# The output stage of a two-layer image kernel: two buffers for its inputs, and the next image's sums among this image's groups

## The reference, cut to what matters

```python
ys = ys + Ds.reshape(1, K_DIRS, d, 1) * xs          # four directions
y = _cross_merge(ys, h, w)                          # flips the reversed two, transposes the column order, adds
y = jnp.transpose(y, (0, 2, 1))                     # pixels first, channels last
mu = jnp.mean(y, -1, keepdims=True)
var = jnp.mean(jnp.square(y - mu), -1, keepdims=True)
y = (y - mu) * jax.lax.rsqrt(var + LN_EPS) * ln_weight + ln_bias
```

## Time and profile before

| | us |
|---|---|
| median of 3 runs | 22312.98 |
| lowest, highest | 22303.36, 22334.86 |
| the profiled execution: its time | 22314.07 |
| the profiled execution: its span | 22312.3 |
| the output stage's part of the span (21397.2 to 22312.3) | 915.1 |

### The profile page before, as it was taken

The page is one execution under the profiler, slowest core; times in us unless marked ns, Lnnn a source line. Parts: engine busy times, 40 slices in busy tenths (PEclk is TensorE's granted clock), DMA queues, the critical chain, the costliest instruction groups (busy, mean ns, idle before and its releaser), DMA issues. The chain is left out here.

```text
span 22312.3 us, 287094 instructions
## 1 busy us (share of the span) xinstructions
PE 16801.2 (75%) x84632; PEld 5876.1 (26%) x84632; DVE 19495.2 (87%) x21108; ACT 9584.4 (43%) x14631; POOL 16107.3 (72%) x5892
## 2 busy tenths in 40 slices
PE   8999999989997777777777777777777777777731
PEld 5555555552221111111111111111111111111111
DVE  5555555559998999999999999999999999999976
ACT  3433433337774444444444444444444444444410
POOL 0000000006667999999999999999999999999977
PEclk9999999999997777777777777777777777766765
DMA  0000000016666666666666666666666666666666
GB/s 20 15 16 16 15 16 15 16 37 226 231 227 154 131 129 126 126 128 128 129 129 131 128 128 126 126 129 130 129 128 128 128 127 125 130 131 129 128 144 163
DMA packets 1129422, 2519.98 MB, mean 113 GB/s; under 512 B 247606, under 2 KB 448824, under 8 KB 1112960
## 3 DMA queue, kind: packets, MB, share of 16 engines
q1 hardware_dynamic: 1128320, 2508.11, 50.2%
HBM read 2000.43 MB, written 507.38 MB: 112 GB/s over the span
## 5 line engine op out<-in xcount | busy, mean ns | idle before, releaser
L1212 POOL TENSOR_TENSOR c_pr<-c_hs,c_c_u 128x1568 f32<-128x1568 f32 x3072 | 10794.1, 3525 | 546.5 <-DVE c_hs L1176 473.0
L1119 ACT ACTIVATE c_psum<-c_dt_u,c_a_neg 128x784 f32<-128x784 f32 x6144 | 5641.7, 918 | 8236.2 <-DVE c_hs L1176 8192.6
L1064 PE MATMUL c_psum<-c_pr,c_red 128*64 128x392 f32 x24576 | 7302.9, 713 | 2.7 <-POOL c_pr L1212 2.7
L1176 DVE TENSOR_TENSOR_SCAN c_hs<-c_psum,c_carry,c_dbx 128x784 f32<-128x784 f32 x3264 | 6347.1, 2025 | 0.0
L1053 PE MATMUL c_psum<-c_br_u,c_sel 48*128 48x512 bf16 (+1 forms) x8704 | 3008.3, 438 | 4148.5 <-DVE c_dbx L1156 4051.7
L1156 DVE TENSOR_TENSOR c_dbx<-c_u_u,c_psum 128x784 f32<-128x784 f32 x4352 | 4857.3, 1116 | 51.7 <-PE c_psum L1053 51.7
L195 POOL TENSOR_TENSOR a_xpb<-a_x_sb,a_pb_sb 98x768 f32<-98x768 f32 x128 | 231.5, 1809 | 4641.0 <-DVE a_x L283 4627.4
L1201 POOL TENSOR_TENSOR c_dbp<-c_u_u,c_bp_u 128x784 f32<-128x784 f32 x1792 | 3334.4, 1861 | 42.3 <-DMA c_c_u<-scr_bc 42.3
L1176 DVE TENSOR_TENSOR_SCAN c_hs<-c_psum,c_carry,c_dbp 128x784 f32<-128x784 f32 x1344 | 2734.2, 2034 | 0.0
L1053 PEld LDWEIGHTS c_psum<-c_br_u,c_sel 48*128 48x128 bf16 x8704 | 524.4, 101 | 8379.4 <-DVE c_dbx L1156 7925.3
L1064 PEld LDWEIGHTS c_psum<-c_pr,c_red 128*64 128x64 f32 x24576 | 1804.3, 178 | 3472.2 <-issue 3188.6
(11 more groups left out here) (117 smaller groups left out, 18555.2 us busy)
## 6 DMA issues: line engine op xcount, KB each, us to landing
c_c_u<-scr_bc SPq DMA_DIRECT2D x512, 1568.0 KB, 28.9
c_dt_u<-scr_dt SPq DMA_DIRECT2D x512, 588.0 KB, 7.4
c_u_u<-scr_u SPq DMA_DIRECT2D x512, 588.0 KB, 11.4
c_bp_u<-scr_bc SPq DMA_DIRECT2D x512, 588.0 KB, 22.2
scr_dt<-p_dt_o SPq DMA_DIRECT2D x384, 392.0 KB, 3.0
scr_u<-p_u_o SPq DMA_DIRECT2D x384, 392.0 KB, 2.4
scr_y<-c_y_sb SPq DMA_DIRECT2D x256, 294.0 KB, 17.8
d_yin<-scr_y SPq DMA_DIRECT2D x32, 2352.0 KB, 14.4
```

The costliest lines, as they stand in the source:

```text
L1064: mm = pe.matmul(Y(3 * w + q)[64 * h:64 * h + 64, :], red[:], pr[:, s % RP, HT * h:HT * h + HT], start=(p == 0 and opens(w)), stop=(p == N ...
L1119: nc.scalar.activation(dA(s), dt_u[:, d, s // NPR, :], ACT.Exp, scale=a_neg[:, k, s:s + 1]).then_inc(exp_done, 1)
L1176: nc.vector.tensor_tensor_scan(hs[:, s % RH, way], dA(s)[:, way], data, init, ALU.mult, ALU.add).then_inc(scan_done, 1)
L1212: nc.gpsimd.tensor_tensor(pr[:, s % RP:s % RP + 2, :], hs[:, s % RH:s % RH + 2, :], c_u[:, d, s % NPR:s % NPR + 2, :], ALU.mult).then_inc( ...
```

## The change

Nothing is computed otherwise. The changes of order and storage are:

- `yin` and `x_in` get a second buffer, by the parity `par` of the image. `yf` is gone: VectorE writes its result in place over plane 0 of `yin`, and TensorE reads it there.
- SP issues both loads of image b+1 at the head of image b's body, behind a wait for the transposes of image b-1 (`t_full`), and then the seven stores of image b. The body is written twice in the loop, once for each parity (`halves`).
- GpSimd's two additions for image b+1 stand behind groups 0 and 2 of image b (`add`), VectorE's two operations for image b+1 behind `normalise(3)` and `normalise(5)` of image b (`with_x`). Those of image 0 stand ahead of everything.
- TensorE waits for the single PSUM banks that it overwrites, and no longer for the whole image before.

```diff
-        yin = sb("yin", [HC, 2, 2, L])
-        x_in = sb("x_in", [HC, 2, L])
-        yf = sb("yf", [HC, 2, L])
+        yin = sb("yin", [HC, 2, 2, 2, L])
+        x_in = sb("x_in", [HC, 2, 2, L])
...
+        def halves(eng, body):
+
+            body(0, 0, False)
+            if n_img > 2:
+                with eng.Fori(0, n_img // 2 - 1) as i:
+                    body(2 * i + 1, 1, False)
+                    body(2 * i + 2, 0, False)
+            body(n_img - 1, 1, True)
...
-            def stores(b):
+            def body(b, par, last):
+                if not last:
+                    if not (isinstance(b, int) and b == 0):
+                        sp.wait_ge(t_full, NGRP * b)
+                    for a in range(2):
+                        load(b + 1, 1 - par, a)
                 for g in range(NGRP):
                     sp.wait_ge(o_done, NGRP * b + g + 1)
                     dst = out[bass.ds(b, 1), TT * GT * g:TT * GT * (g + 1), :].rearrange("u (t p) c -> p (u t) c", p=TT)
                     sp.dma_start(dst, ob[:, g].rearrange("p (t c) -> p t c", t=GT)).then_inc(o_out[g], 16)
 
-            load(0, 0)
-            load(0, 1)
-            if n_img > 1:
-                with sp.Fori(0, n_img - 1) as b:
-                    for a in range(2):
-                        sp.wait_ge(yf_done, 2 * b + a + 1)
-                        load(b + 1, a)
-                    stores(b)
-            stores(n_img - 1)
+            load(0, 0, 0)
+            load(0, 0, 1)
+            halves(sp, body)
...
-            def body(b, first):
-                for a in range(2):
-                    pool.wait_ge(y_in[a], 48 * b + 48)
...
+            def add(b, par, a):
+                pool.wait_ge(y_in[par][a], 24 * (b - par) + 48)
+                rows = yin[:, par, a, 0].rearrange("p (h w) -> p h w", h=IMG)
+                nc.gpsimd.tensor_tensor(rows, rows, yin[:, par, a, 1].rearrange("p (w h) -> p h w", h=IMG),
+                                        ALU.add).then_inc(add_done, 1)
+
+            def body(b, par, last):
                 for g in range(NGRP):
...
                     nc.gpsimd.tensor_tensor(o, o, b_sb[:].unsqueeze(1).to_broadcast([TT, GT, C]), ALU.add).then_inc(o_done, 1)
+                    if not last and g in (0, 2):
+                        add(b + 1, 1 - par, g // 2)
...
-                    if a == 0 and not first:
-                        dve.wait_ge(t_full, NGRP * b)
-                    nc.vector.scalar_tensor_tensor(yf[:, a], x_in[:, a], dsum[:, a:a + 1], yin[:, a, 0],
-                                                   ALU.mult, ALU.add).then_inc(yf_done, 1)
+            def with_x(b, par, a):
+                dve.wait_ge(add_done, 2 * b + a + 1)
+                y = yin[:, par, a, 0]
+                nc.vector.scalar_tensor_tensor(y, x_in[:, par, a], dsum[:, a:a + 1], y, ALU.mult, ALU.add).then_inc(yf_done, 1)
...
                     stat(g)
                     if g:
                         normalise(g - 1)
+                    if not last and g in (4, 6):
+                        with_x(b + 1, 1 - par, g // 2 - 2)
                 normalise(NGRP - 1)
...
-                    elif not first and g < 4:
-                        pe.wait_ge(nm_done, NGRP * b)
+                    elif not (isinstance(b, int) and b == 0):
+                        pe.wait_ge(nm_done, n - (2 if g < 3 else 6))
```

More of the change, by code:

```diff
@@ L1248, in build_output @@
         c_in = sem("d_c_in")
-        y_in = [sem("d_y_in0"), sem("d_y_in1")]
+        y_in = [[sem(f"d_y_in{par}{a}") for a in range(2)] for par in range(2)]
         ready = sem("d_ready")
@@ L1266, in _, with load @@
                 sp.dma_start(dst, src).then_inc(c_in, 16)
-            def load(b, a):
-                sp.dma_start(yin[:, a], ysc[bass.ds(2 * b, 2), a].rearrange("u p t -> p u t")).then_inc(y_in[a], 16)
+            def load(b, par, a):
+                arrived = y_in[par][a]
+                sp.dma_start(yin[:, par, a], ysc[bass.ds(2 * b, 2), a].rearrange("u p t -> p u t")).then_inc(arrived, 16)
                 top = SHIFT * IMG
-                sp.dma_start(x_in[:, a, top:L], xn[a, :, bass.ds(b * L + top, L - top)]).then_inc(y_in[a], 16)
-                sp.dma_start(x_in[:, a, 0:top], xn[a, :, bass.ds(b * L + L, top)]).then_inc(y_in[a], 16)
-            def stores(b):
+                sp.dma_start(x_in[:, par, a, top:L], xn[a, :, bass.ds(b * L + top, L - top)]).then_inc(arrived, 16)
+                sp.dma_start(x_in[:, par, a, 0:top], xn[a, :, bass.ds(b * L + L, top)]).then_inc(arrived, 16)
+            def body(b, par, last):
[4 more added lines that the diff above has]
+                        load(b + 1, 1 - par, a)
                 for g in range(NGRP):
@@ L1303, in _ @@
                 pool.sem_inc(o_out[g], 16)
-            def body(b, first):
-                for a in range(2):
-                    pool.wait_ge(y_in[a], 48 * b + 48)
-                    rows = yin[:, a, 0].rearrange("p (h w) -> p h w", h=IMG)
-                    nc.gpsimd.tensor_tensor(rows, rows, yin[:, a, 1].rearrange("p (w h) -> p h w", h=IMG),
-                                            ALU.add).then_inc(add_done, 1)
+            def add(b, par, a):
[4 more added lines that the diff above has]
+            def body(b, par, last):
                 for g in range(NGRP):
@@ L1317, in body @@
                     nc.gpsimd.tensor_tensor(o, o, b_sb[:].unsqueeze(1).to_broadcast([TT, GT, C]), ALU.add).then_inc(o_done, 1)
-            images(pool, body)
+                    if not last and g in (0, 2):
+                        add(b + 1, 1 - par, g // 2)
+            add(0, 0, 0)
+            add(0, 0, 1)
+            halves(pool, body)
         @block.vector
@@ L1326, in _, with body @@
             dve.wait_ge(ready, 2)
[L1328 to L1331, removed]
-                    if a == 0 and not first:
-                        dve.wait_ge(t_full, NGRP * b)
-                    nc.vector.scalar_tensor_tensor(yf[:, a], x_in[:, a], dsum[:, a:a + 1], yin[:, a, 0],
-                                                   ALU.mult, ALU.add).then_inc(yf_done, 1)
+            def with_x(b, par, a):
+                dve.wait_ge(add_done, 2 * b + a + 1)
+                y = yin[:, par, a, 0]
+                nc.vector.scalar_tensor_tensor(y, x_in[:, par, a], dsum[:, a:a + 1], y, ALU.mult, ALU.add).then_inc(yf_done, 1)
+            def body(b, par, last):
+                first = isinstance(b, int) and b == 0
                 def stat(g):
@@ L1362, in body @@
                         normalise(g - 1)
+                    if not last and g in (4, 6):
+                        with_x(b + 1, 1 - par, g // 2 - 2)
                 normalise(NGRP - 1)
-            images(dve, body)
+            with_x(0, 0, 0)
+            with_x(0, 0, 1)
+            halves(dve, body)
         @block.scalar
@@ L1380, in body @@
                     nc.scalar.activation(rstd[:, g], lnv[:, g], ACT.Exp, scale=-0.5).then_inc(rs_done, 1)
-            images(act, body)
+            halves(act, body)
         @block.tensor
@@ L1398, in body @@
                             tok = TT * (GT * g + t)
-                            mm = pe.transpose(tile_ps(g, t)[:, HC * a:HC * a + HC], yf[:, a, tok:tok + TT], id_sb[:])
+                            mm = pe.transpose(tile_ps(g, t)[:, HC * a:HC * a + HC], yin[:, par, a, 0, tok:tok + TT], id_sb[:])
                     mm.then_inc(t_full, 1)
-            images(pe, body)
+            halves(pe, body)
 def build(nc, ins, out, n_img):
```

## The result

| | before | changed |
|---|---|---|
| median, us | 22305.45 (6 runs) | 22434.76 (6 runs) |
| lowest to highest, us | 22276.27 to 22334.86 | 22416.42 to 22466.75 |
| ratio to before, 95% interval | | 1.006, 1.0047 to 1.0073 |
| profiled execution: time, span | 22314.07, 22312.3 | 22440.55, 22438.7 |
| output stage, from SP's first DMA to the end | 915.1 | 1048.9 |

The changed kernel is slower by 129 us of median; in the profiled executions the output stage is 133.8 us longer, and the three stages ahead of it ended 7.4 us earlier (21389.81 against 21397.19). The forecast was 22435 us.

The account below looks back on a forecast made before the run. The output stage was taken as bound by a loop through TensorE and GpSimd. Late load (L 20.0 us), additions, groups and two blocks made a 64.6 us period against 55.36, +122.1 us in all: 22435 us, range 22388 to 22466.

Parts of the forecast that it names:

- What goes: Output stage: GpSimd no longer waits for VectorE at an image's start; alone, the period would fall by 13.2 us.
- What becomes late: Loads queue on SP behind the previous image's seven stores, so GpSimd idles 16.4 us an image.
- L: Time from an image's last GpSimd group to the start of the next addition: 20.0 us, bounds 19.3 and 21.3.
- The blocks: VectorE's whole-image operation holds GpSimd's second group operation for 3.06 us, twice an image, 6.1 us.
- the proportion taken from prep's casts: In prep a cast ran 0.74 us longer beside a VectorE operation's 0.83 us; scaled to L1334's 3.28 us.
- The second half: The load's second half lands 15.8 us behind the first, GpSimd needs it after 18.7 us: no cost.
- The sum: Output stage: period 64.6 us, 9.3 us more than 55.36; difference +122.1 us in all.
- A free exclusion: Rival: VectorE loses every conflict, the blocks cost GpSimd nothing; period 58.5 us, total 22344 us; chance 0.04.
- one that is paid once an image: Rival: only one of the two blocks an image costs GpSimd time; total 22390 us; chance 0.04.
- A load at the stores' rate: Rival: loads reach 371 GB/s instead of 224, L is 14 us, total 22352 us; chance 0.04.
- A load that delays something else: Rival: stores stand behind 7 MB of loads on the new load queue; 22470 to 22500 us; chance 0.04.
- The faster case: Rival: loads come in time, GpSimd waits for nothing, period 48.3 us, total 22206 us; chance 0.04.

Follow-up runs that it names:

- e1: Against the changed kernel, SP issues the loads for image b+2 between the stores of groups 2 and 3 of image b; 22205.3 us, ratio 0.9948.
- e3: Against the changed kernel, GpSimd's two additions for the next image stand behind groups 3 and 5 instead of 0 and 2; 22304.0 us, ratio 0.9991.
- e4: Against the changed kernel, x has its own semaphores: GpSimd's addition waits for y alone, VectorE's operation for x; 22376.33 us, ratio 1.0028.
- e7: Against the changed kernel, SP's loads for image b+2 stand one group earlier, between the stores of groups 5 and 6; 22377.14 us, ratio 1.0034.
- e2: Against the changed kernel, ScalarE makes x times dsum and the sum with y is left out; 22359.04 us, ratio 1.0018.
- e6: Against the changed kernel: loads between stores 0 and 1, addition waits for y alone, group work split over VectorE, ScalarE, GpSimd; 22082.21 us, ratio 0.9898.

## Why the prediction was right

*What goes.* VectorE stayed ahead, as reckoned: GpSimd waited for it once, at the start (10.1 us).

*What becomes late.* L was forecast as 20.0 us. It is 22037.88 - 22017.36 = 20.52 us in the image shown, and 17.11 + 3.64 = 20.75 us on average over the 14 images. The issue came after 1.12 us, not 0.8, and the third piece landed 18.3 us later, where the forecast had 17.5 and up to 0.9 for the store ahead. e1, e3, e4 and e7 move the load or the demand for it and find this cost each time.

*The blocks.* Forecast 3.06 us, 30 of them. Measured (293.9 - 201.8) / 30 = 3.07 us. e2 removes their cause and they go; the proportion taken from prep's casts held for an operation four times as long. The Trainium skill's rule (SBUF — State Buffer, "Who interferes with whom") is that the first to start has the shared pair of ports for its whole instruction and the other is blocked. The trace agrees: VectorE's operation waits for the multiply and takes 5.00 us instead of 3.48, and GpSimd's next operation waits for VectorE's and takes 4.88 us instead of 1.80.

*The second half* landed in time: GpSimd never waited for it behind image 0, with 18.65 us between the two additions. The forecast that without the block it would be on the edge is borne out by e2: the additions are 15.6 us apart there, and once in 14 images the second one waits, for 0.20 us.

*The sum.* The forecast for the stage was +122.1 us, of which 14 periods longer by 9.3 us are the bulk; measured +133.8. The difference lies in the period: the second addition for image 1 starts at 21468.17 and the last of the stage at 22384.0, so 14 periods have a mean of 65.42 us, not 64.6, which is 11 us. Nearly all of it is L, 0.75 us more on average than forecast, 14 times. That the medians agree to 1 us is luck: the forecast stood on a median before of 22312.98 us and a difference of 122.1 us, and the later runs gave 22305.45 us and 129.3 us. The base came out 7.5 us lower, the cost 7.2 us higher, and the two cancel. In the profiled executions the like happened: the stages ahead ended 7.4 us earlier in the changed kernel, so that its span is only 126.4 us longer.

*Rivals.* A free exclusion (22344 us) and one that is paid once an image (22390 us) are refuted by the 30 long L1319 and by e2. A load at the stores' rate (22352 us) is refuted by the 18.3 us: from 22022 to 22037, with the loads first in the queues, the DMA engines were busy all the time and moved 231 GB/s. The Trainium skill (DMA: Bandwidth & Descriptors, "Specifications") gives about 358 GB/s as the limit between HBM and one core; the loads stayed far below it, which does not contradict a limit but makes it no price for them. Why loads move slower than stores is not shown. A load that delays something else (22470 us and more) is out as well: GpSimd waited for VectorE only at the start. The faster case needed a load ahead of the stores, and e1 shows that this one condition was indeed all it lacked. Forecast for it were 107 us under the kernel before (22206 against 22312.98), measured 113.

## What to carry to other kernels

A second buffer allows an early load, it doesn't make one: read what stands ahead of the load in the issuing engine's program, here seven waits of the previous image, and count from the last of them to the point of use. When work is moved forward in time, its loads must move by as much, or the engine waits as long as before, only for a load instead of another engine. And where GpSimd has become the bound, a VectorE operation with two SBUF inputs can be charged to it at nearly full length (here 3.07 of 3.48 us), even if VectorE has time to spare.

## What was not expected of the hardware

VectorE can hold up a long operation of GpSimd too. In the earlier trace rows the whole-image addition ran at its usual length and VectorE's operation waited. In e6 (timeline of VectorE, then of GpSimd) VectorE's operation started first:

```profile
21821.96 3.90 DVE L1343 SCALAR_TENSOR_TENSOR d_yin<-d_x_in,d_dsum,d_yin 96x3136 f32<-96x3136 f32 x1
```

```profile
21822.53 11.53 POOL L1316 TENSOR_TENSOR d_yin<-d_yin 96x3136 f32<-96x3136 f32 x1
```

The addition took 11.53 instead of 8.35 us, so the cost to GpSimd is 3.2 us, about the same for an operation of 1.80 us and for one of 8.35 us. On the other hand, VectorE's reads of `w_sb` together with PSUM, one SBUF input, took 1.36 to 1.39 us for four, less than the 1.60 us of the operation that they replace, and GpSimd's operation beside them kept its 1.80 us.

The recorded lengths of unchanged instructions in the scan stage differ between the two profiled executions (VectorE's L1176 with two further inputs 2025 against 1832 ns, mean of 3264) although the stage took as long in both: from its first L1176 to the output stage 14476.9 and 14474.7 us. Why the recorded lengths differ is open. A mean length from one execution is no evidence by itself that a kernel's time changed.
